# Third stage of a four-stage transformer chain: how half of the attention weights are turned, and when they meet the values

## The chip, the cores and the metric

The kernel runs on one core of one Trainium2 chip. The metric is the device time of one execution in microseconds (us), the median of several. The core has a matrix engine (TensorE, PE), a vector engine (VectorE, DVE), a scalar engine (ScalarE, ACT), a general engine (GpSimd, POOL) and a queue that issues the transfers (SyncE, SP). Each works through its own list of instructions in order and waits on semaphores for the others.

## The reference, cut to what matters

2048 tokens (16 x 128) of width 512 pass through four stages, each of the form x = x + gate * block(layernorm(x)): a latent attention, a gated FFN with low-rank experts, a causal attention, and a mixture of low-rank maps. The change lies in the third:

```python
def _L1_xattn_ref(q, latent_kv, Wq, Wkv_expand, Wout):      # q: layernorm(x); 16 heads of 32
    qp = q @ Wq.T
    k, v = jnp.split(latent_kv @ Wkv_expand.T, 2, axis=-1)
    scores = jnp.einsum('bhqd,bhkd->bhqk', qh, kh) * inv_sqrt_d
    scores = jnp.where(causal, scores, jnp.finfo(scores.dtype).min)
    attn = jax.nn.softmax(scores, axis=-1)
    out = jnp.einsum('bhqk,bhkd->bhqd', attn, vh)
    return out @ Wout.T
```

Each of the 16 sequences has 128 tokens, so the scores of a head and a sequence are one 128x128 square. The value product needs that square with the keys on the partitions, that is, turned.

## The kernel before, in words

The tokens are worked in four tiles m of 512 (four sequences b each). In the third stage the 16 heads are four groups g of four heads j, and a **unit** u = 4m + g is one group of heads for one tile: 16 units. The stage is a loop over u from 0 to 17 that stands in each engine's program, with the work of unit u spread over passes u to u + 2. What one pass u holds, in TensorE's order:

- `scores3(u-1)`: 16 small products into banks 4 to 7 (one bank a head, four sequences in it). The causal mask must be in the bank first. In the passes after u = 3, 4, 5, 6, 10 and 14 (and the first ones) TensorE puts it there itself with 4 products (`mkb,idb` in the profile). For the others it is "seeded": ACT or DVE copies it into the bank as soon as its exponentials are done (`seed3`, `seeded(u)`).
- `q3(u)` (12 products), then in passes 6, 10, 14 `v3(m)` (12), then the output projection of finished tokens, `wo3`, 12 products a block: one block where g = 3 or 1, two where g = 0 (`wo_at(u)`; from pass 7).
- `turn3(u-2)`: 16 transpositions of P, head by head, into four banks taken from the ring of banks 0 to 3 (`ring3`); then `k3(u)` (3 products), `ln_turn` (transpositions of the next tokens) and `cx_turn`.
- `av3(u-2)`: the value product, 16 small products on PT3, the copy of the turned P in SBUF.

The other engines in the same pass. DVE: `largest(u-1, j)`, four maxima straight from the score banks; `q3_out(u)`; the low half of `av3(u-3)`; two `inverse`; seeds of heads 0 and 1 (where g = 1, head 0 alone); `v3`; `final3` for each `wo3` block; `turn3` copies of heads 0 and 1; `inverse`; `k3(u)`; `ln_pre`, `ln_turn` and `cx_turn` low halves; the last `inverse`. ACT: `exp3(u-1)`, 16 exponentials (four a head), the remaining seeds, `turn3` copies of heads 2 and 3 (ahead of the last head's exponentials or of its seed), `ln_turn` and `cx_turn` high halves, the high half of `av3(u-2)`. POOL: `norm3(u-1, j)`, which multiplies P by the inverse sums, `rstd_of`, `ln_norm` (the layer norm of tokens for the next tile) and `w4_split`. SP: loads of tokens and of the fourth stage's weights (`w4`, through six slots of the staging buffer STG), loads and stores of the third stage's output rows.

`scores3(u)` waits for `q3` and `k3` of its unit to be copied out (Q3 and K3 are single buffers), and for the score banks to be free, which the last exponential or the last seed does. No planner is involved: the order is written out in each engine's function. In the trace all products carry line 118 and transpositions 121, copies 127 (DVE, POOL) and 124 (ACT), `largest` 146, `inverse` 149, `ln_pre` 152, 155 and 136, `ln_norm` 137, 32x32 block turns 164, transfers 170. MSK holds Q3 and K3, PTV holds PT3 and the values, AR and XT the split operands.

The first stage already turns its P in another way: DVE turns every 32x32 block (line 164), the result goes to the DRAM scratch `pscr` and comes back with the blocks moved by four transfers (PYZ is the buffer at both ends).

## Time and profile before

| | us |
|---|---|
| median of 3 runs | 1375.35 (1373.85 to 1378.79) |
| the profiled execution | 1376.7 |
| its span in the trace | 1374.9, so 1.8 lie around it |
| third stage, passes 1 to 17 | from about 1028 to 1223 |
| PE, DVE, ACT, POOL busy over the span | 98%, 68%, 38%, 31% |
| granted TensorE clock | 0.997 of full |

The scores of each pass start in the trace at these times (from pass 4 on the pass is full; 17 has none, and its first product starts at 1212.10):

| pass | 3 | 4 | 5 | 6 | 7 | 8 | 9 | 10 | 11 | 12 | 13 | 14 | 15 | 16 |
|---|---|---|---|---|---|---|---|---|---|---|---|---|---|---|
| us | 1049.01 | 1059.53 | 1068.96 | 1078.60 | 1091.15 | 1102.30 | 1115.49 | 1126.27 | 1138.79 | 1149.92 | 1163.09 | 1173.88 | 1186.38 | 1197.09 |

A busy share is an average over stages with different limits. For the third stage the table by stretches, one a pass, and the chain of waits say more than the shares of the whole span.

### The profile page before, as it was taken

Reading aid. Unit: us, or ns where it says so; the run is one execution under the profiler, and the core shown is the slowest. Engines: PE = TensorE matmul, PEld = TensorE weight load, DVE = VectorE, ACT = ScalarE, POOL = GpSimd, SP = SyncE. Lnnn points to the kernel's source line nnn. Section 1 sums busy time; section 2 is a strip of 40 time slices with the busy share of each in tenths; the row PEclk is TensorE's granted clock in tenths of the full one; section 3 lists DMA queues with packets and bytes.
Section 4 is the critical chain, followed back from the end, with each engine's and each line's share of the span. In section 5 each row is a group of like instructions: output and inputs, shape, how many; then the busy total and the mean of one; then the engine's idle time right before and its main releaser. Section 6 shows DMA issues by size and latency. Waiting matters only on the chain.

```text
span 1374.9 us, 20467 instructions
## 1 busy us (share of the span) xinstructions
PE 1348.0 (98%) x7596; PEld 1091.5 (79%) x7596; DVE 929.3 (68%) x1787; ACT 518.5 (38%) x1569; POOL 422.1 (31%) x463
## 2 busy tenths in 40 slices
PE   7899999999999999999999999999999999999999
PEld 6688888888778788878887888788876788887787
DVE  5565675666674877786678667776988777845533
ACT  2544455445464331231113111311127777822220
POOL 3123433233254443101111112113427865630000
PEclk9999999999999999999999999999999999999999
DMA  8633434433454322210121112112334031144431
GB/s 282 222 124 101 148 124 130 131 123 116 135 149 120 92 85 77 88 47 20 43 88 31 51 39 85 43 46 69 106 102 136 28 129 62 47 139 153 139 123 54
DMA packets 108615, 138.35 MB, mean 101 GB/s; under 512 B 12876, under 2 KB 66252, under 8 KB 108516
## 3 DMA queue, kind: packets, MB, share of 16 engines
q1 hardware_dynamic: 108516, 137.05, 31.3%
q8 instruction: 60, 0.98, 0.3%
q14 instruction: 39, 0.32, 0.1%
HBM read 97.15 MB, written 39.85 MB: 100 GB/s over the span
## 4 chain that ended last, share of the span: by engine, by line
PE 81%; DVE 9%; DMA 5%; ACT 2%; issue 1%; SPq 1%; POOL 1%; DVEq 0%; ACTq 0%; POOLq 0%
PE bank L118 78%; PE bank L121 4%; DMA PYZ<-pscr 2%; DMA pscr<-PYZ 2%; SPq L170 1%; DVE PYZ L164 1%; DVE XR L140 1%; DVE AH L130 1%; DVE STG L130 1%; DVE AH L127 1%; DVE st L152 1%; ACT Pb L124 1%; ACT PT L124 1%; DMA XR<-scr 0%; DVE XR L137 0%
## 5 line engine op out<-in xcount | busy, mean ns | idle before, releaser
L118 PE MATMUL bank<-XT,AR 128*128 128x512 f32 x1152 | 280.2, 393 | 0.1
L118 PE MATMUL bank<-AR 128*128 128x512 f32 x1056 | 260.6, 396 | 3.2 <-DVE Msb L127 2.3
L118 PEld LDWEIGHTS bank<-XT,AR 128*128 128x128 f32 x1152 | 213.9, 188 | 48.3 <-issue 1.5
L124 ACT ACTIVATE STG<-bank,b1c 128x512 f32<-128x512 f32 x128 | 88.3, 690 | 387.7 <-PE bank L118 317.7
L118 PEld LDWEIGHTS bank<-AR 128*128 128x128 f32 x1056 | 193.7, 188 | 48.2 <-DVE Msb L127 2.7
L118 PE MATMUL bank<-AR,CT 128*128 128x512 f32 x768 | 192.7, 394 | 0.0
L118 PE MATMUL bank<-AR,AH 128*128 128x512 f32 x768 | 185.9, 390 | 0.0
L127 DVE CAST AH<-STG 128x512 fp32r<-128x512 f32 x192 | 93.8, 488 | 110.5 <-PE bank L118 96.4
L118 PEld LDWEIGHTS bank<-AR,AH 128*128 128x128 f32 x768 | 143.7, 188 | 30.7 <-issue 1.1
L118 PEld LDWEIGHTS bank<-AR,CT 128*128 128x128 f32 x768 | 140.0, 188 | 27.2 <-issue 0.4
L127 POOL CAST BA<-STG 128x256 fp32r<-128x256 f32 x64 | 31.4, 490 | 396.4 <-PE bank L118 242.8
L130 DVE TENSOR_TENSOR AH<-STG,AH 128x512 fp32r<-128x512 f32 x192 | 140.5, 732 | 6.6
L124 ACT ACTIVATE Pb<-bank,sm 128x128 f32<-128x128 f32 x256 | 90.0, 377 | 122.3 <-DVE sm L136 122.3
L130 POOL TENSOR_TENSOR Pb<-Pb,sm 128x512 f32<-128x512 f32 x64 | 66.6, 1042 | 185.3 <-DVE sm L149 185.3
L118 PE MATMUL bank<-TM,BA 128*128 128x512 f32 x384 | 107.5, 392 | 1.0 <-POOL BA L130 0.4
L124 ACT ACTIVATE P<-bank,sm 128x128 f32<-128x128 f32 x256 | 90.1, 395 | 31.9 <-DVE sm L146 31.9
L118 PE MATMUL bank<-AH,BA 128*128 128x512 f32 x384 | 97.5, 389 | 0.0
L130 POOL TENSOR_TENSOR rstd<-ve,mhalf 128x1 f32<-128x1 f32 x64 | 49.1, 771 | 148.6 <-DVE ve L136 148.5
L130 DVE TENSOR_TENSOR STG<-STG 128x512 f32<-128x512 f32 x128 | 89.6, 700 | 4.2
L130 POOL TENSOR_TENSOR P<-P,sm 128x512 f32<-128x512 f32 x64 | 65.4, 1043 | 75.8 <-DVE sm L149 75.8
L118 PEld LDWEIGHTS bank<-TM,BA 128*128 128x128 f32 x384 | 71.4, 188 | 19.0 <-ACT STG L124 2.2
L118 PEld LDWEIGHTS bank<-AH,BA 128*128 128x128 f32 x384 | 72.1, 188 | 15.4
(139 smaller groups left out, 1839.3 us busy)
## 6 DMA issues: line engine op xcount, KB each, us to landing
XR<-scr SPq DMA_DIRECT2D x64, 256.0 KB, 2.9
pscr<-PYZ SPq DMA_DIRECT2D x30, 512.0 KB, 2.9
PYZ<-pscr SPq DMA_DIRECT2D x120, 128.0 KB, 2.9
XR<-in_x_dram SPq DMA_DIRECT2D x32, 256.0 KB, 3.6
scr<-XR SPq DMA_DIRECT2D x32, 256.0 KB, 2.1
STG<-in_WoT_dram SPq DMA_DIRECT2D x8, 512.0 KB, 3.9
STG<-in_Wq_dram SPq DMA_DIRECT2D x8, 512.0 KB, 4.9
STG<-in_W1L_dram SPq DMA_DIRECT2D x16, 256.0 KB, 2.7
```

The lines of the kernel that those rows point to most:

```text
L118: return self.e.matmul(o, w, x, start=start, stop=stop, skip_group_check=True) if self.e else Nothing()
L121: return self.e.transpose(o, x, ident) if self.e else Nothing()
L124: return self.e.activation(o, x, func, **kw) if self.e else Nothing()
L127: return self.e.tensor_copy(o, x) if self.e else Nothing()
L130: return self.e.tensor_tensor(out=o, in0=a, in1=b, op=op) if self.e else Nothing()
L140: return self.e.scalar_tensor_tensor(out=o, in0=a, scalar=s, in1=b, op0=op0, op1=op1) if self.e else Nothing()
L152: return self.e.bn_stats(o, x) if self.e else Nothing()
L164: return self.e.transpose(o, x) if self.e else Nothing()
L170: return self.e.dma_start(o, x) if self.e else Nothing()
```

## The change

1. Heads 0 and 1 of each unit are no longer turned by TensorE. At the start of DVE's pass u, ahead of the maxima, `turn_p3(u-2)` turns the 32x32 blocks of P of both heads into P3Y, 1024 columns of the staging buffer (it waits there for `norm3` of both). SP stores P3Y to `pscr` and loads it back in four transfers into P3Z, the first 1024 columns of PTV. The load waits for the value product of the unit before, since P3Z is single, and both stand at the start of SP's pass, ahead of its other transfers.
2. TensorE's and DVE's `turn3` keep 8 transpositions a unit and none of the copies of heads 0 and 1; ACT's two copies remain, and stand ahead of the last head's exponentials in passes 6, 10 and 14 as elsewhere.
3. The value product of unit u-3 (`av3(u-3)`) is issued in pass u behind `q3(u)`, before it was that of unit u-2 at the end of pass u. ACT takes its high half behind the exponentials of heads 0 and 1, DVE its low half behind the seeds. For heads 0 and 1 it reads P3Z in four runs of 32 columns.
4. The two token tiles (2, 1, 0) and (2, 1, 1) are normalised by DVE in pass 2 in place of POOL in pass 1.
5. P3Y takes the place of two weight slots, so the `w4` loads rotate over four.

```diff
+        P3Y, P3Z = STG[:, 2048:3072], PTV[:, 0:1024].rearrange("p (j n c) -> p n j c", j=4, n=8)
...
             def turn3(u, ring):
-                for b in range(4):
+                for b in (2, 3):
...
             def av3(u, ring):
                 for b in range(4):
-                    pe.wait_ge(*ps.drained(("pt3", u, b)))
                     pe.wait_ge(*ps.drained(("v3", m, b)))
+                pe.wait_ge(*d_p3[u, 3])
+                pe.wait_ge(*ps.drained(("pt3", u, 2)))
+                pe.wait_ge(*ps.drained(("pt3", u, 3)))
...
+                        if j < 2:
+                            ins = pe.matmul(o.rearrange("p (a c) -> p a c", a=4), V3[:, b, 32 * h:32 * h + 32],
+                                            P3Z[:, 4 * j + b], True, True)
...
             # TensorE, pass u
                 if 1 <= u < 16:
                     q3(u, ring3)
+                if u >= 3:
+                    av3(u - 3, ring3)
...
-                if u >= 2:
-                    av3(u - 2, ring3)
+            av3(15, ring3)
...
             # ScalarE, pass u
                 if 1 <= u <= 16:
                     exp3(u - 1, (0, 1))
+                if u >= 3:
+                    av3(u - 3)
...
             # VectorE
+            def turn_p3(u):
+                for j in range(2):
+                    e.wait_ge(*nm3_ok[u, j])
+                    if u:
+                        e.wait_ge(*t_p3[u - 1])
+                    e.turn(blocks_out(P3Y)[:, 4 * j:4 * j + 4],
+                           blocks_in(P3[:, u % 2, 0:1024])[:, 4 * j:4 * j + 4]).then_inc(*p3y_ok.mark((u, j)))
...
+                if u >= 2:
+                    turn_p3(u - 2)
                 if 1 <= u <= 16:
                     for j in range(4):
                         largest(u - 1, j)
...
+                if u == 2:
+                    ln_norm(2, 1, 0)
+                    ln_norm(2, 1, 1)
...
-                if u >= 2:
-                    turn3(u - 2, 0)
-                    turn3(u - 2, 1)
...
             # SyncE
+            def p3_store(u):
+                e.wait_ge(*p3y_ok[u, 1])
+                if u >= 2:
+                    e.wait_ge(*d_p3[u - 2, 3])
+                e.dma(pscr[u % 2], P3Y).then_inc(*t_p3.mark(u))
+
+            def p3_load(u):
+                e.wait_ge(*t_p3[u])
+                if u:
+                    e.wait_ge(*ps.full(("av", u - 1)))
+                src = pscr[u % 2].rearrange("(j r) (i x) -> i r j x", j=4, i=4)
+                for k in range(4):
+                    e.dma(PTV[32 * k:32 * k + 32, 0:1024].rearrange("r (j x) -> r j x", j=4), src[k]).then_inc(*d_p3.mark((u, k)))
```

TensorE, passes 8 (g = 0) and 9 (g = 1) up to the scores of pass 10, before:

```order
700 L118 MATMUL bank<-MSK 128x128 x16
701 L118 MATMUL bank<-AR 128x512 x36
702 L121 MATMUL bank<-ident,P 128x128 x16
703 L118 MATMUL bank<-AR 128x512 x3
704 L118 MATMUL bank<-PTV 32x128 x16
705 L118 MATMUL bank<-MSK 128x128 x16
706 L118 MATMUL bank<-AR 128x512 x24
707 L121 MATMUL bank<-ident,P 128x128 x16
708 L118 MATMUL bank<-AR 128x512 x3
709 L121 MATMUL bank<-ident,XR 128x128 x4
710 L118 MATMUL bank<-PTV 32x128 x16
711 L118 MATMUL bank<-MSK 128x128 x16
```

The same, now:

```order
701 L118 MATMUL bank<-MSK 128x128 x16
702 L118 MATMUL bank<-AR 128x512 x12
703 L118 MATMUL bank<-PTV 32x128 x16
704 L118 MATMUL bank<-AR 128x512 x24
705 L121 MATMUL bank<-ident,P 128x128 x8
706 L118 MATMUL bank<-AR 128x512 x3
707 L118 MATMUL bank<-MSK 128x128 x16
708 L118 MATMUL bank<-AR 128x512 x12
709 L118 MATMUL bank<-PTV 32x128 x16
710 L118 MATMUL bank<-AR 128x512 x12
711 L121 MATMUL bank<-ident,P 128x128 x8
712 L118 MATMUL bank<-AR 128x512 x3
713 L121 MATMUL bank<-ident,XR 128x128 x4
714 L118 MATMUL bank<-MSK 128x128 x16
```

The value product (PTV) stood between `k3` (the x3) and the scores (MSK); now `k3` stands next to the scores of the next pass where g = 0, and the value product lies behind `q3`.

VectorE, the second half of pass 9 up to the maxima of pass 10, before (MSK at line 127 is the copy of `k3`, lines 152 to 136 the statistics of `ln_pre`):

```order
1170 L127 COPY PTV<-bank 128x512 x2
1171 L149 RECIPROCAL sm<-sm 128x4
1172 L127 COPY MSK<-bank 128x512
1173 L152 BN_STATS st<-XR 128x6
1174 L155 BN_AGGR mv<-st 128x2
1175 L136 TENSOR_SCALAR ve<-mv 128x1
1176 L152 BN_STATS st<-XR 128x6
1177 L155 BN_AGGR mv<-st 128x2
1178 L136 TENSOR_SCALAR ve<-mv 128x1
1179 L130 TENSOR_TENSOR AR<-bank,AR 128x4x128
1180 L149 RECIPROCAL sm<-sm 128x4
1181 L146 TENSOR_REDUCE sm<-bank 128x4 x4
```

The same, now:

```order
1172 L149 RECIPROCAL sm<-sm 128x4
1173 L127 COPY MSK<-bank 128x512
1174 L152 BN_STATS st<-XR 128x6
1175 L155 BN_AGGR mv<-st 128x2
1176 L136 TENSOR_SCALAR ve<-mv 128x1
1177 L152 BN_STATS st<-XR 128x6
1178 L155 BN_AGGR mv<-st 128x2
1179 L136 TENSOR_SCALAR ve<-mv 128x1
1180 L130 TENSOR_TENSOR AR<-bank,AR 128x4x128
1181 L149 RECIPROCAL sm<-sm 128x4
1182 L164 STREAM_TRANSPOSE STG<-P 128x4x4x32 x2
1183 L146 TENSOR_REDUCE sm<-bank 128x4 x4
```

Two copies went from the middle of the pass, and two block turns came in between the last inverse and the next maxima.

ScalarE, pass 9 (mkb is a seed, PTV a copy of the turned P), before and then now:

```order
314 L124 ACTIVATE P,sm<-bank,sm 128x128 x16
315 L124 ACTIVATE bank<-mkb 128x512 x2
316 L124 ACTIVATE PTV<-bank 128x512 x2
317 L124 ACTIVATE bank<-mkb 128x512
318 L124 ACTIVATE XT<-bank 128x4x128
319 L124 ACTIVATE AR<-bank 128x512
```

```order
321 L124 ACTIVATE P,sm<-bank,sm 128x128 x8
322 L124 ACTIVATE AR<-bank 128x512
323 L124 ACTIVATE P,sm<-bank,sm 128x128 x8
324 L124 ACTIVATE bank<-mkb 128x512 x2
325 L124 ACTIVATE PTV<-bank 128x512 x2
326 L124 ACTIVATE bank<-mkb 128x512
327 L124 ACTIVATE XT<-bank 128x4x128
```

The high half of the value product (AR, 128x512) moved from the end of the pass into the middle of the exponentials, ahead of the seeds.

## Rows read from the trace of the kernel before

**Rows 1.** The page's first part: busy time, share of the span, instructions.

```profile
PE 1348.0 (98%) x7596; PEld 1091.5 (79%) x7596; DVE 929.3 (68%) x1787; ACT 518.5 (38%) x1569; POOL 422.1 (31%) x463
```

**Rows 2.** Stretches of passes 8, 9, 11: length, busy PE, PEld, DVE, ACT, POOL.

```profile
1102.30:1115.49 13.19, 13.09 (x124) 10.79 (x120) 9.61 (x19) 8.37 (x37) 5.98 (x6) 1.00 0.24 85
1115.49:1126.27 10.78, 10.78 (x115) 9.03 (x111) 8.55 (x20) 9.32 (x39) 8.55 (x8) 1.00 0.24 78
...
1137.83:1149.92 12.09, 12.09 (x123) 9.75 (x120) 9.68 (x20) 9.45 (x39) 8.32 (x8) 1.00 0.19 70
```

**Rows 3.** TensorE by time, pass 9: start, us, line, operation, count, idle before.

```profile
1115.49 1.17 PE L118 MATMUL bank<-MSK 32*128 32x128 f32 x32
1116.59 3.04 PE L118 MATMUL bank<-XT,AR 128*128 128x512 f32 x12
1119.47 2.89 PE L118 MATMUL bank<-AR 128*128 128x512 f32 x12
1122.19 1.91 PE L121 MATMUL bank<-ident,P 128*128 128x128 f32 x16
1123.87 0.96 PE L118 MATMUL bank<-AR 128*128 128x512 f32 x3
...
1125.26 1.08 PE L118 MATMUL bank<-PTV 128*32 128x128 f32 x32
1126.27 1.17 PE L118 MATMUL bank<-MSK 32*128 32x128 f32 x32
```

**Rows 4.** ScalarE by time, pass 9.

```profile
1117.40 0.37 ACT L124 ACTIVATE P<-bank,sm 128x128 f32<-128x128 f32 x1 [1.19 <-DVE sm L146]
...
1122.91 1.21 ACT L124 ACTIVATE bank<-mkb 128x512 f32<-128x512 bf16 x2
1123.95 1.17 ACT L124 ACTIVATE PTV<-bank 128x512 f32<-128x512 f32 x2
1124.90 0.70 ACT L124 ACTIVATE bank<-mkb 128x512 f32<-128x512 bf16 x1
1125.42 0.70 ACT L124 ACTIVATE AR<-bank 128x512 fp32r<-128x512 f32 x1
```

**Rows 5.** VectorE by time, pass 9 and the maxima of pass 10.

```profile
1116.68 2.48 DVE L146 TENSOR_REDUCE sm<-bank 128x4 f32<-128x512 f32 x4 [0.49 <-PE bank L118]
...
1123.13 1.28 DVE L127 COPY PTV<-bank 128x512 f32<-128x512 f32 x2
...
1124.86 0.69 DVE L127 COPY MSK<-bank 128x512 f32<-128x512 f32 x1 [0.37 <-PE bank L118]
1125.47 0.68 DVE L152 BATCH_NORM_STATS2 st<-XR 128x6 f32<-128x512 f32 x1
...
1128.16 2.45 DVE L146 TENSOR_REDUCE sm<-bank 128x4 f32<-128x512 f32 x4
```

**Rows 6.** VectorE by time, first stage: the same two block turns.

```profile
54.19 1.30 DVE L164 STREAM_TRANSPOSE PYZ<-Pb 128x512 f32<-128x512 f32 x2
```

**Rows 7.** TensorE by time: first and last scores of the table, two early waits.

```profile
1046.47 0.63 PE L121 MATMUL bank<-ident,XR 128*128 128x128 f32 x4 [1.44 <-POOL XR L137]
...
1049.01 1.17 PE L118 MATMUL bank<-MSK 32*128 32x128 f32 x32
...
1065.05 1.09 PE L121 MATMUL bank<-ident,P 128*128 128x128 f32 x8 [0.51 <-DVE AR L130]
...
1197.09 1.17 PE L118 MATMUL bank<-MSK 32*128 32x128 f32 x32
```

**Rows 8.** Layer norm instructions (line 137), whole span: ns least/median/most.

```profile
L137 DVE TENSOR_SCALAR XR<-XR,mv,rstd x48: 504/539/1568, 6.0 to 1302.6; 128x512 f32<-128x512 f32 x48
L137 POOL TENSOR_SCALAR XR<-XR,mv,rstd x16: 2079/2084/2092, 1042.2 to 1188.3; 128x512 f32<-128x512 f32 x16
```

**Rows 9.** Chain of waits, first stage, an early unit: start, us, what.

```profile
41.59 6.09 DMA pscr<-PYZ
...
49.02 2.92 DMA PYZ<-pscr
```

**Rows 10.** The tile PYZ and its scratch: time to landing of all transfers.

```profile
DMA to landing us min/median/max: 2.4/2.9/6.9
```

More of the change, by code:

```diff
@@ L353, in build @@
         t_ly = sig("t_ly", 16)
+        t_p3, d_p3 = sig("t_p3", 16), sig("d_p3", 16)
         def kinds(count, names):
@@ L363, in build @@
         vy_ok, vz_ok, py_ok, pz_ok, ly_ok, lz_ok = kinds(on_dve, "vy_ok vz_ok py_ok pz_ok ly_ok lz_ok")
+        (p3y_ok,) = kinds(on_dve, "p3y_ok")
         c_mh, c_sel, rs_ok, kvc_rd, kvr_ok, kvl_ok = kinds(on_pool, "c_mh c_sel rs_ok kvc_rd kvr_ok kvl_ok")
@@ L412, in build, with normed_by_pool @@
                 xr_take("ln", 3, m, tb)
-        normed_by_pool = ((2, 1), (2, 2), (2, 3), (3, 0))
+        def normed_by_pool(ph, m, tb):
+            return (ph, m) in ((2, 1), (2, 2), (2, 3), (3, 0)) and (ph, m, tb) not in ((2, 1, 0), (2, 1, 1))
         def xr_ap(*key):
@@ L562, in ln_turn @@
                 pe.wait_ge(*ps.free(key))
-                pe.wait_ge(*(xp_ok if (ph, m) in normed_by_pool else xn_ok)[ph, m, tb])
+                pe.wait_ge(*(xp_ok if normed_by_pool(ph, m, tb) else xn_ok)[ph, m, tb])
                 for c in range(4):
@@ L986, in av3 @@
                         h = 4 * g + j
-                        ins = pe.matmul(k[32 * j:32 * j + 32, 128 * b:128 * b + 128], V3[:, b, 32 * h:32 * h + 32],
-                                        PT3[:, 512 * j + 128 * b:512 * j + 128 * b + 128], True, True)
+                        o = k[32 * j:32 * j + 32, 128 * b:128 * b + 128]
+                        if j < 2:
+                            ins = pe.matmul(o.rearrange("p (a c) -> p a c", a=4), V3[:, b, 32 * h:32 * h + 32],
+                                            P3Z[:, 4 * j + b], True, True)
+                        else:
+                            ins = pe.matmul(o, V3[:, b, 32 * h:32 * h + 32],
+                                            PT3[:, 512 * j + 128 * b:512 * j + 128 * b + 128], True, True)
                 ins.then_inc(*ps.fill(("av", u)))
@@ L1388, in exp3 @@
                     if u >= 2:
-                        ac.wait_ge(*ps.full(("pt3", u - 2, j)))
+                        ac.wait_ge(*(p3y_ok[u - 2, j] if j < 2 else ps.full(("pt3", u - 2, j))))
                     for b in range(4):
@@ L1421, in h4 @@
                         ac.wait_ge(*ps.full(("pt3", 14, 3)))
+                        ac.wait_ge(*p3y_ok[14, 1])
                         ac.wait_ge(*d_c4[3])
@@ L1445, in scalar @@
                     turn3(u - 2, 3)
+                if values:
+                    exp3(u - 1, (3,))
                 if seeded(u):
@@ L1456, in scalar @@
                     cx_turn(m + 1)
-                if u >= 2:
-                    av3(u - 2)
+            av3(15)
             def logits(m):
@@ L1890, in inverse @@
                 e.recip(S[:, 4:8], S[:, 4:8]).then_inc(*rc_ok.mark(("3", u, j)))
-            def turn3(u, b):
-                e.wait_ge(*ps.full(("pt3", u, b)))
-                if u:
-                    e.wait_ge(*ps.full(("av", u - 1)))
-                e.copy(PT3[:, 512 * b:512 * b + 512], ps.ap(("pt3", u, b))[:, :]).then_inc(*ps.drain(("pt3", u, b), on_dve))
+            def turn_p3(u):
[5 more added lines that the diff above has]
+                           blocks_in(P3[:, u % 2, 0:1024])[:, 4 * j:4 * j + 4]).then_inc(*p3y_ok.mark((u, j)))
             def av3(u):
@@ L1928, in vector @@
                         seed3(u, j)
+                if u >= 3:
+                    av3(u - 3)
                 if u > 4 and g == 2:
@@ L2198, in w4_split @@
                 kind, c, hi, lo, _ = w4[n]
-                e.wait_ge(*d_slot[n % 6]["w4", n])
+                e.wait_ge(*d_slot[n % 4]["w4", n])
                 if kind == "U":
                     e.wait_ge(*ps.full(("w3", 2, 3)))
-                split(hi, lo, slots[n % 6]).then_inc(*w4_ok.mark((kind, c)))
+                split(hi, lo, slots[n % 4]).then_inc(*w4_ok.mark((kind, c)))
             for u in range(18):
@@ L2216, in gpsimd @@
                         rstd_of(2, 1, tb)
-                    for tb in tiles3(u)[g]:
-                        ln_norm(2, 1, tb)
                 for n in w4_step.get(u, ()):
@@ L2449, in xf_store @@
                 e.dma(rows(3, m, tb), XF[:, tb, :]).then_inc(*t_xf[tb].mark(m))
+            def p3_store(u):
[10 more added lines that the diff above has]
+                    e.dma(PTV[32 * k:32 * k + 32, 0:1024].rearrange("r (j x) -> r j x", j=4), src[k]).then_inc(*d_p3.mark((u, k)))
             for u in range(18):
                 m, g = divmod(u, 4)
+                if u >= 2:
+                    p3_store(u - 2)
+                    p3_load(u - 2)
                 for tile in (ln3_tiles(u) if u < 16 else ()):
@@ L2457, in sync @@
                 for n in w4_step.get(u, ()):
-                    if n >= 6:
-                        e.wait_ge(*w4_ok[w4[n - 6][0:2]])
+                    if n >= 4:
+                        e.wait_ge(*w4_ok[w4[n - 4][0:2]])
                     elif n < 2:
@@ L2463, in sync @@
                         e.wait_ge(*ps.drained(("acc2", 3, 3)))
-                    e.dma(slots[n % 6], w4[n][4]).then_inc(*d_slot[n % 6].mark(("w4", n)))
+                    e.dma(slots[n % 4], w4[n][4]).then_inc(*d_slot[n % 4].mark(("w4", n)))
                 if u > 4 and g == 2:
```

5 lines of the change are left out of this document (removed).

## The prediction

> **What bounds the kernel now.** TensorE is busy 98% of the span [rows 1]. I read the third stage by stretches next: a pass of 13.19 us holds 13.09 of TensorE, one of 10.78 holds 10.78, one of 12.09 all of it, with DVE, ACT and POOL at 8 to 10 [rows 2]. So on paper it is TensorE's, and what is taken from it counts in full. But the busy times of ACT and DVE hide that they form a loop with TensorE, and how close that loop is decides this case. In pass 9 it runs: scores at 1115.49 [rows 3]; maxima 1.19 later, at 1116.68 [rows 5]; exponentials from 1117.40, 0.72 behind the maxima, to 1122.91, so 5.51 for 16; two seeds 1.04; two copies of the turned P 0.95; the last seed from 1124.90 to 1125.60 [rows 4]. Only then are the banks free for the next scores, which start at 1126.27 [rows 3]: the loop has 0.67 us to spare. Here the next maxima start 1.89 behind their scores, not 1.19 [rows 5]: DVE is late already.
>
> **What TensorE is relieved of.** 16 transpositions take 1122.19 to 1123.87, 1.68 us; seen with what follows, 0.105 each [rows 3]. Eight fewer give 0.84 a unit, 13.4 for 16 units. The value product (1.01, from 1125.26 to 1126.27 [rows 3]) moves and stays the same length if four runs of 32 columns stream like one of 128. No row shows that form: at the least it costs nothing, at the most each of the 8 small products takes twice as long, 0.5 a unit or 8 in all. I take nothing, since even at contiguous P 32 of these small steps take 1.08 [rows 3], so they run side by side and one that reads slower has cover. Two waits lie in passes 2 to 4 too: 1.44 for POOL's layer norm, and 0.5 in each of three passes for the bank of the value product [rows 7]; both lose their cause, 1.4 and 1.5. Were TensorE the bound throughout, the gain would be 13.4 + 2.9 = 16.3.
>
> **What is put on the loop.** On DVE the two copies (1.28) leave the middle of the pass [rows 5], where they shortened no wait; two block turns, 1.30 [rows 6], come in directly ahead of the maxima. As work this is even; as a place it is not. On ACT the high half of the value product, about 0.5 (the like instruction at 1125.42 is one [rows 4]), comes from the end of the pass into the loop. And TensorE's value product no longer stands between `k3` and the next scores: the copy of `k3` ends at 1125.55, 1.68 behind the start of `k3` at 1123.87 [rows 3, 5], and the scores need it.
>
> The Trainium skill (page VectorE: DVE Perf Modes, "The three transpose paths" and the rules for kernel authors) advises TensorE for a 128x128 transposition whose target may be PSUM, and VectorE for 32x32 blocks; it gives 390 ns against 311 for bf16. The rows differ from that as a choice for this kernel: 105 ns of TensorE's path against 1.30 / 8 = 163 ns of DVE for a square. An estimate from its figures would have a unit give 3.1 us back for 2.5 on DVE, over 16 units some 50 us less on TensorE, which no row here bears out; the trace decides, 0.84 for 1.3.
>
> **The loop worked out.** Let L be the start of the maxima, F the time when the score banks are free. In a pass with g = 1 and seeds, F = L + 0.72 + 5.51 + 0.5 + 1.04 + 0.95 + 0.7 = L + 9.4. With g = 3 one seed less, L + 8.9. In passes 3 to 5, without seeds, L + 7.7; where `v3` is (6, 10, 14) ACT has two more copies, L + 8.8; in both the scores start at F + 0.3, behind TensorE's own mask, else at F + 0.1. The next L: after F, ACT takes the high half of the turned tokens (0.6, 1.1 or 1.6 for one, two or three tiles), DVE the low half (0.65), the inverse (0.1) and now the block turns (1.3): F + 2.65, 3.1 or 3.6, and F + 1.45 with no tile. The earliest L is 1.19 behind the scores. With g = 0 and seeds (8, 12) TensorE has two projection blocks and ACT waits for it: `k3` starts 11.1 behind the scores before, + 1.0 - 0.84 = 11.3 now, the copy ends at 13.0, and that is the pass; 13.19 before [rows 2]. The next L stands behind that copy by 1.0 for one tile's statistics (2.69 for two of them, a low half and an inverse, from 1125.47 to 1128.16 [rows 5]), 0.1 and 1.3: 2.4 after the scores.
>
> Carried through, from the pass table, scores after against before: pass 3 at 1048.05 (-1.0: the waits of pass 2 go, the last exponential then bounds it), 4 at 1058.8 (-0.8), 5 at 1070.1 (+1.1, since three turned tiles made pass 4's maxima late), 6 at 1079.7 (+1.1), 7 at 1091.2 (0), 8 at 1103.0 (+0.7), 9 at 1116.0 (+0.5), 10 at 1127.9 (+1.6), 11 at 1139.6 (+0.8), 12 at 1151.4 (+1.5), 13 at 1164.4 (+1.3), 14 at 1176.3 (+2.4), 15 at 1188.0 (+1.6), 16 at 1199.8 (+2.7) [first and last of before in rows 7]. One of these in full: pass 9 starts at 1116.0, L = 1118.4, F = 1127.8, scores at 1127.9, against 10.78 a pass before; pass 10: L = 1127.8 + 2.65 = 1130.5, F = 1139.3, scores at 1139.6, where TensorE before needed 12.5 for masks, `v3` and turns: what pass 9 loses, pass 10 gives back in part. Passes 16 and 17 have no scores behind them and are TensorE's: -0.84 each. Sum: +2.7 - 1.7 = **+1.0 us**.
>
> **What stays hidden.** The layer norm on DVE, 0.5 each and 1.57 at worst against 2.08 on POOL [rows 8], lies in pass 2 and is in the -1.0; at worst it takes that back. The worst is a row beside a busy POOL, and the Trainium skill (SBUF — State Buffer, "A bandwidth-pool intuition that's wrong") has it that one of the two blocks fully while the other holds the shared port; the trace agrees (504 to 1568 ns for one form). The transfers: store 6.1 at most in the chain, four issues about 1.4, landing 2.9, together 10.4 [rows 9]; from L to the value product of the next pass there are 11.5 in pass 3 and 13 to 15 later. SP's other transfers now stand behind `p3_load`, some 5 us into the pass; what they load is wanted one pass later. The slots fall from six to four, but a slot is reused four passes later, after its split. The last unit: its turns lie at about 8 in pass 16, landed at 19, wanted at 23.
>
> **Rivals.** *TensorE stays the bound.* If L is not late (POOL and ACT tails shorter than I add them), g = 1 gives 10.65, g = 2 and 3 save 0.9 each and g = 0 0.2, two of the early passes 1 each: -7 to -10, to the full -16.3: 1359 to 1368. For it: TensorE's busy share; against it: `inverse` of the last head and the low halves stand ahead of the turns in DVE's list, and maxima already start late. *The transfers are late.* Slower: the landing ranges up to 6.9 [rows 10], which makes the way 6.1 + 1.4 + 6.9 = 14.4; the point from which it decides is 13.4 in a full pass and 11.5 in passes 3 to 5. At 14.4 twelve passes wait 1.0 and three 2.9: +20, 1396; with half of them late +10, 1386. Against it: the median is 2.9. *POOL holds the turns.* They wait for `norm3` of two heads, and POOL has two layer norms (2.08 each [rows 8]) and a weight split in some passes; where it is behind, DVE waits ahead of the maxima. Under 0.2 a pass it is lost in the sum; at 0.75 in each of the 11 passes that the loop bounds it is +8, 1384. *The change does nothing here* is the forecast itself: the gain is made on TensorE and lost behind the maxima.
>
> **How the numbers follow.** The span goes from 1374.9 to 1375.9; with 1.8 around it 1377.7 against the profiled 1376.7. That execution was 1.35 above the median, so I put the forecast at 1375.35 + 1.0 = 1376.4. Chances: the loop as worked out 0.52 (its own range, 0.35 a pass either way over 14 passes, 1371 to 1381), TensorE bound 0.28, the two slower ones 0.10 each. Half a per cent, about what a measurement can tell here, is 6.9 us: faster 0.28, same 0.52, slower 0.20. The range takes in 1364 to 1385.
>
> **What would show it.** After: passes of 11.5 to 12 us with g = 1 and 3, of 13.0 with g = 0; TensorE idle ahead of scores, released by ACT's seed or the `k3` copy; maxima 2 to 3 us behind their scores; busy TensorE down by some 13 while the span stands. TensorE without idle time, or maxima at 1.2, would make it wrong on the fast side; a value product that waits for a transfer into PTV, on the slow side.

## The result, and the profile after

| kernel | median of the time | runs | ratio to before, 95% interval |
|---|---|---|---|
| before | 1376.08 us | 7 | |
| changed | 1383.02 us (1381.25 to 1384.89) | 7 | 1.0050 (1.0037 to 1.0064) |

The changed kernel is 6.9 us slower. Its profiled execution has a span of 1381.2 us, 6.3 more than before's 1374.9. The page's busy line of the changed kernel, to be read beside [rows 1]:

```profile
PE 1339.4 (97%) x7468; PEld 1077.7 (78%) x7468; DVE 929.5 (67%) x1789; ACT 516.1 (37%) x1569; POOL 418.2 (30%) x461
```

TensorE is busy 8.6 us less and ends 6.3 us later: it idles some 15 us more. Passes 8, 9 and 11 of the changed kernel, each from its scores to the next (length, then busy PE, PEld, DVE, ACT, POOL). They stand against [rows 2], whose third row, though, begins with the masks ahead of pass 11's scores; from scores to scores pass 11 took 11.13 us before:

```profile
1105.39:1118.77 13.38, 12.44 (x111) 9.82 (x112) 9.88 (x20) 9.21 (x39) 5.96 (x6) 1.00 0.52 179
1118.77:1130.47 11.70, 10.08 (x104) 8.07 (x104) 9.25 (x22) 8.95 (x39) 8.54 (x8) 1.00 0.47 158
1142.45:1154.00 11.55, 10.74 (x109) 8.46 (x108) 9.07 (x18) 8.83 (x40) 7.33 (x7) 1.00 0.60 213
```

Before, TensorE was busy 10.78 of 10.78 us in pass 9. Now it is busy 10.08 of 11.70. What ends its idle time there, TensorE by time in pass 9 of the changed kernel (compare [rows 3]):

```profile
1118.77 1.17 PE L118 MATMUL bank<-MSK 32*128 32x128 f32 x32 [0.87 <-DVE MSK L127]
1119.88 3.01 PE L118 MATMUL bank<-XT,AR 128*128 128x512 f32 x12
1122.82 1.08 PE L118 MATMUL bank<-PTV 128*32 128x128 f32 x32
1123.83 3.02 PE L118 MATMUL bank<-AR 128*128 128x512 f32 x12
1126.69 1.03 PE L121 MATMUL bank<-ident,P 128*128 128x128 f32 x8
1127.48 0.94 PE L118 MATMUL bank<-AR 128*128 128x512 f32 x3
1128.25 0.60 PE L121 MATMUL bank<-ident,XR 128*128 128x128 f32 x4
1130.47 0.79 PE L118 MATMUL bank<-MSK 32*128 32x128 f32 x17 [1.61 <-ACT bank L124]
```

Two waits stand there that were not there before: the scores that begin the pass wait 0.87 for VectorE's copy of the keys (K3, tile MSK), and the scores that end it 1.61 for ScalarE's seed of a score bank. VectorE ahead of those scores, and ScalarE at the end of the same pass (compare [rows 4, 5]):

```profile
1117.93 0.69 DVE L127 COPY MSK<-bank 128x512 f32<-128x512 f32 x1 [0.66 <-PE bank L118]
...
1119.63 1.28 DVE L164 STREAM_TRANSPOSE STG<-P 128x512 f32<-128x512 f32 x2
1120.83 2.44 DVE L146 TENSOR_REDUCE sm<-bank 128x4 f32<-128x512 f32 x4
```

```profile
1127.50 1.22 ACT L124 ACTIVATE bank<-mkb 128x512 f32<-128x512 bf16 x2
1128.54 1.18 ACT L124 ACTIVATE PTV<-bank 128x512 f32<-128x512 f32 x2
1129.49 0.72 ACT L124 ACTIVATE bank<-mkb 128x512 f32<-128x512 bf16 x1
1130.01 0.71 ACT L124 ACTIVATE AR<-bank 128x512 fp32r<-128x512 f32 x1
```

The maxima start 2.06 us behind their scores (1.19 before), directly behind the block turns. The last seed is out 9.4 us behind the start of the maxima, and the scores start at 9.6. The four largest waits of TensorE over the third stage (1036.9 to 1228.1) of the changed kernel, 16.2 of 18.4 us: what waited, for whom, sum, times, longest:

```profile
PE bank L118 <- ACT P L124: 6.3, 7, 2.0
PE bank L118 <- ACT bank L124: 5.4, 5, 1.6
PE bank L121 <- ACT PTV L124: 2.7, 4, 1.3
PE bank L118 <- DVE MSK L127: 1.8, 2, 0.9
```

Before, the same view of its third stage has three entries, 3.6 us together:

```profile
PE bank L121 <- DVE AR L130: 1.5, 3, 0.5
PE bank L121 <- POOL XR L137: 1.4, 1, 1.4
PE bank L118 <- DVE PTV L127: 0.7, 1, 0.7
```

The transfers are no part of this. No wait names them, and they land as those of the first stage do (compare [rows 10]); the page's rows of issues, with median us to landing:

```profile
pscr<-STG SPq DMA_DIRECT2D x16, 512.0 KB, 2.6
PTV<-pscr SPq DMA_DIRECT2D x64, 128.0 KB, 2.8
```

One more thing happened, in pass 5. TensorE by time, and then four stretches of it (the number ahead of the DMA share is the granted clock, 1.00 being the 2.4 GHz level and 0.50 the 1.2 GHz level):

```profile
1067.64 0.39 PE L118 MATMUL bank<-mkb,idb 128*128 128x512 bf16 x1 [1.03 <-ACT P L124]
1070.01 0.39 PE L118 MATMUL bank<-mkb,idb 128*128 128x512 bf16 x1 [1.98 <-ACT P L124]
1070.33 1.67 PE L118 MATMUL bank<-MSK 32*128 32x128 f32 x32
1071.93 4.11 PE L118 MATMUL bank<-AR 128*128 128x512 f32 x12
```

```profile
1068.00:1070.00 2.00, 0.03 (x1) 0.00 (x0) 1.32 (x5) 1.96 (x10) 0.92 (x1) 1.00 0.96 287
1071.00:1072.00 1.00, 1.00 (x21) 0.78 (x17) 0.38 (x2) 0.00 (x0) 0.90 (x3) 0.50 0.00 0
1073.00:1074.00 1.00, 1.00 (x4) 0.81 (x3) 1.00 (x3) 1.00 (x7) 1.00 (x2) 0.50 0.59 217
1075.00:1076.00 1.00, 1.00 (x9) 0.55 (x8) 0.00 (x0) 0.63 (x4) 0.94 (x1) 1.00 0.00 0
```

After two waits of 1.03 and 1.98 us the clock fell to the lower level for about 3.4 us: the scores took 1.67 instead of 1.17, the query products 4.11 instead of 3.02, so 1.6 us were lost on top of the wait. It is not a matter of this one execution: behind the same wait of 1.98 us ahead of pass 5 the clock fell in the profiles of experiments 2, 3 and 8 too, and not in that of 5. The kernel before has no fall in its third stage.

### The profile page after: what moved, and what is told of

It reads as the page before. It is cut to its first block, busy times and chain, and to the rows that moved or that the text cites. A ratio compares the mean times of both kernels' runs of the same rounds, so it can differ in the third digit from the quotient of the medians.

```text
span 1381.2 us, 20251 instructions
## 1 busy us (share of the span) xinstructions
PE 1339.4 (97%) x7468; PEld 1077.7 (78%) x7468; DVE 929.5 (67%) x1789; ACT 516.1 (37%) x1569; POOL 418.2 (30%) x461
## 4 chain that ended last, share of the span: by engine, by line
PE 73%; DVE 10%; ACT 8%; DMA 5%; issue 2%; SPq 1%; POOL 0%; DVEq 0%; ACTq 0%; POOLq 0%
PE bank L118 72%; ACT P L124 4%; PE bank L121 2%; DMA PYZ<-pscr 2%; SPq L170 1%; DMA pscr<-PYZ 1%; ACT PTV L124 1%; DVE PYZ L164 1%; DVE XR L140 1%; DVE AH L130 1%; DVE STG L130 1%; DVE STG L164 1%; DVE st L152 1%; ACT Pb L124 1%; DVE AH L127 1%
```

## The experiments

All are read by two measures. The time (median, ratio to before) decides what is faster. But one profile scatters: the scores of pass 2 start between 1032.9 and 1038.9 us, and from the first logits of stage four to the end it is 151.5 to 156.7 us. So the mechanism is read from the **third stage** of each profile, in two parts: from the scores of pass 2 to those of pass 16, and from there to the first logits. That is 160.05 + 26.14 us before and 165.69 + 25.39 in the changed kernel. The last columns are the lengths of four passes of the steady part. Each ratio is to runs of the kernel before made beside that experiment; their medians lie between 1375.34 and 1376.18. All in us:

| kernel | time | ratio (95%) | passes 2 to 15 | 16 to logits | pass 8 | 9 | 10 | 11 |
|---|---|---|---|---|---|---|---|---|
| before | 1376.08 | | 160.05 | 26.14 | 13.19 | 10.78 | 12.52 | 11.13 |
| changed | 1383.02 | 1.0050 (1.0037 to 1.0064) | 165.69 | 25.39 | 13.38 | 11.70 | 11.98 | 11.55 |
| 1 product moved alone | 1381.10 | 1.0037 (1.0021 to 1.0052) | 163.87 | 27.21 | 14.14 | 11.42 | 12.51 | 11.43 |
| 2 without transfers | 1382.29 | 1.0054 (1.0034 to 1.0073) | 167.88 | 25.39 | 13.39 | 11.69 | 11.98 | 11.54 |
| 3 turns a pass earlier | 1384.60 | 1.0060 (1.0044 to 1.0076) | 169.77 | 25.39 | 13.38 | 11.72 | 13.59 | 10.74 |
| 4 idle time filled once | 1383.25, one run | | 165.68 | 25.37 | 13.39 | 11.69 | 13.59 | 11.54 |
| 5 turns last | 1375.96 | 1.0005 (0.9992 to 1.0018) | 157.51 | 29.66 | 13.38 | 11.34 | 12.00 | 10.63 |
| 6 turns last, keys first | 1373.53 | 0.9983 (0.9967 to 0.9999) | 150.69 | 29.97 | 13.26 | 10.38 | 11.30 | 10.42 |
| 7 keys first | 1377.43 | 1.0015 (1.0002 to 1.0028) | 159.36 | 25.72 | 13.53 | 10.71 | 12.21 | 10.78 |
| 8 norms back | 1382.81 | 1.0055 (1.0036 to 1.0073) | 167.43 | 25.39 | 13.38 | 11.67 | 11.98 | 11.53 |
| 9 as 6, trimmed | **1366.06** | **0.9927 (0.9908 to 0.9946)** | 149.85 | 25.52 | 12.46 | 10.37 | 11.53 | 10.41 |
| 10 no turns, keys first | 1393.66 | 1.0126 (1.0106 to 1.0146) | 174.51 | 27.17 | 14.58 | 12.31 | 13.56 | 12.68 |
| 11 as 10, key copy early | 1375.56 | 0.9996 (0.9984 to 1.0008) | 158.59 | 27.16 | 13.22 | 10.87 | 12.49 | 11.36 |
| 12 as 9, norms back | 1369.67 | 0.9943 (0.9928 to 0.9959) | 153.07 | 25.52 | 13.38 | 10.39 | 11.35 | 10.41 |

### 1. The value product moved alone

The kernel before, with the product's new place on TensorE, ScalarE and VectorE; all sixteen squares stay on TensorE. As in the change, ScalarE's two copies of turned P stand ahead of the last head's exponentials in passes 6, 10 and 14 too; passes 10 and 14 keep their lengths within 0.01 us, and pass 6 is 0.19 shorter, so this is not what costs time. TensorE's part:

```diff
                 if 1 <= u < 16:
                     q3(u, ring3)
+                if u >= 3:
+                    av3(u - 3, ring3)
...
-                if u >= 2:
-                    av3(u - 2, ring3)
+            av3(15, ring3)
```

> The kernel before with one part of the change: the value product of unit u-3 behind q3 of pass u on TensorE, its halves on ScalarE and VectorE at the places of the change; all 16 transpositions and copies stay, no block turns, no transfers. Loop theory: what hurts is the block turns ahead of the maxima; the move alone exposes the copy of k3 in passes 8 and 12 (+0.65 each), and puts 0.5 on ScalarE's loop, whose maxima are early again without the turns: +1 to +3 us on before. Rival (the move itself is the loss): +6 to +7, as much as the whole change.

Measured: +5.4 us over the 1375.73 of before beside it, third stage 191.08, as long as the changed kernel's. TensorE's three largest waits in it:

```profile
PE bank L118 <- DVE MSK L127: 3.1, 5, 0.9
PE bank L121 <- POOL XR L137: 1.4, 1, 1.4
PE bank L118 <- ACT P L124: 1.2, 2, 0.8
```

The product used to stand between the key product and the next scores, and hid VectorE's copy of the keys. Without it the copy is exposed, 3.1 us. And pass 16 to the logits takes 27.21 against 26.14, 1.07 more: one value product more lies behind the last scores. The expectation of +1 to +3 was too low. So the move alone costs 4.9 us of the third stage, though the maxima of pass 9 start 1.16 us behind their scores, early. What the rest of the change adds there, block turns above all, is zero on balance in these two profiles.

### 2. No transfers

The changed kernel, with the block turns written to two buffers that the value product reads directly. The 80 transfers are left out, and so is their work of putting the blocks of two heads in place.

```diff
-                pe.wait_ge(*d_p3[u, 3])
+                pe.wait_ge(*p3y_ok[u, 1])
...
-                if u >= 2:
-                    p3_store(u - 2)
-                    p3_load(u - 2)
```

> The change without its 80 transfers: the block turns write two buffers in turn and the value product reads them as they are, so the blocks of heads 0 and 1 stand at the wrong places in the sum and the output differs; every other instruction is kept. Loop theory: nothing waited for a transfer into PTV, so the third stage takes the same time, 0 to -1.5 us on the change (the fourth stage's start may be a little earlier): 1381.5 to 1383. Rival (the transfers, or the traffic and SP's queue behind them, are the loss): about 7 back, 1376.

Measured: 1382.29, and passes 8 to 11 are those of the changed kernel to 0.01 us. Passes 2 to 15 are 2.2 us longer in this profile; the clock was at its lower level for about 3.5 us in each of passes 3, 5 and 14, and pass 14 took 13.59 us instead of 12.00. The transfers cost the changed kernel nothing that can be seen.

### 3. The turns one pass earlier

```diff
-                if u >= 2:
-                    turn_p3(u - 2)
...
+                if 1 <= u <= 16:
+                    turn_p3(u - 1)
```

The new call stands behind the layer norm's statistics and ahead of the low halves, where I took VectorE for idle.

> The change with one thing moved: VectorE's block turns of a unit stand one pass earlier, behind the statistics and ahead of the low halves of the turned tokens, where VectorE waits for ScalarE anyway, and not ahead of the maxima. Same instructions on every engine. Loop theory: 1.2 us leaves the loop in some ten passes; passes with g = 1 fall from 11.7 to about 10.8, with g = 3 from 11.6 to about 10.4, with g = 2 to TensorE's own 11.7, g = 0 stays 13.3: third stage 10 to 14 us shorter than in the change, time 1368 to 1373. Rival (VectorE's work counts, not its place): 1383 as the change.

Measured: 1384.6, where 1368 to 1373 had been expected. The turns were still ahead of the maxima (maxima 2.5 us behind their scores in pass 10), and now they could meet P before GpSimd had normalised it. VectorE's wait for that:

```profile
DVE STG L164 <- POOL P L130: 4.8, 5, 3.0
```

Passes 7, 11 and 15 did get 0.5 to 0.8 us shorter. What was lost lies in pass 2 (2.1 us longer), pass 4 (2.9) and pass 10, where the clock fell behind a wait of 1.63. I take it that the end of the pass is not where VectorE has time, but the middle, while the exponentials run; experiment 5 tries that.

### 4. TensorE kept busy ahead of pass 5

The changed kernel with twelve repeated mask products in the idle time ahead of pass 5's scores.

```diff
+                        if u == 4 and j in (1, 2):
+                            for _ in range((0, 4, 8)[j]):
+                                pe.matmul(blocks3(ks[0]), idb[:, :], mask3, True, False)
```

> The change with 12 repeated mask products into a bank that holds only its mask, in the 3 us of pass 4 to 5 in which TensorE stood idle. Theory of the clock: behind that idle time the granted clock fell to 0.50 for about 4 us and the scores and q3 of pass 5 took 1.67 and 4.11 us where they take 1.17 and 3.02 elsewhere; with the engine kept busy the clock stays at 1.00 there, q3 takes 3.0, and pass 5 is 1.5 to 2 us shorter. Rival (the slow q3 comes from operands or the transfers at that time): q3 still takes 4.1.

Measured: the scores took 1.17, the query products 3.02 and pass 5 9.95 us instead of 11.53, so 1.58 of that pass was the clock. But the third stage is as long as ever. In pass 2 the clock fell too, which pass 3 gave back, and pass 10 took 13.59 instead of 11.98:

```profile
1127.60 1.17 PE L118 MATMUL bank<-MSK 32*128 32x128 f32 x32 [1.60 <-ACT bank L124]
1128.70 4.61 PE L118 MATMUL bank<-XT,AR 128*128 128x512 f32 x12
```

```profile
1130.00:1131.00 1.00, 1.00 (x3) 0.73 (x3) 1.00 (x3) 0.22 (x1) 1.00 (x3) 0.50 0.00 0
```

The clock fell behind the idle time of another pass. The changed kernel's profile has the same wait there (1.61) and no fall. So the loss to the clock is real, but its place changes, and filling one gap doesn't cure it: there are others. This rests on one execution.

### 5 to 7. The order of the pass

Experiment 5 moves the turns of the changed kernel behind the query copy (`q3_out`), experiment 7 puts TensorE's key product ahead of the remaining transpositions of P and ScalarE's two copies behind its last exponential and seed, and 6 does both. No run separates the two moves of 7.

VectorE, in 5 and 6:

```diff
-                if u >= 2:
-                    turn_p3(u - 2)
                 if 1 <= u <= 16:
                     for j in range(4):
                         largest(u - 1, j)
                 if 1 <= u < 16:
                     q3_out(u)
+                if u >= 2:
+                    turn_p3(u - 2)
```

TensorE, in 6 and 7:

```diff
+                if 0 < u < 16:
+                    k3(u, ring3)
                 if u >= 2:
                     turn3(u - 2, ring3)
-                if 0 < u < 16:
-                    k3(u, ring3)
```

ScalarE, in 6 and 7:

```diff
+                if 1 <= u <= 16 and not project:
+                    exp3(u - 1, (3,))
+                if seeded(u):
+                    seed3(u, 3)
                 if u >= 2:
                     turn3(u - 2, 2)
                     turn3(u - 2, 3)
-                if values:
-                    exp3(u - 1, (3,))
-                if seeded(u):
-                    seed3(u, 3)
-                if 1 <= u <= 16 and not project and not values:
-                    exp3(u - 1, (3,))
```

> The changed kernel with one edit: VectorE's eight block turns of unit u-2 stand behind the third query copy of unit u (at the end of the pass) and no longer ahead of unit u's maxima. Nothing else is moved. Theory A (the pass is a loop maxima, exponentials, score banks free, next scores; the turns' 1.30 us lie in front of the maxima only where VectorE comes late to them, and behind the query copy they lie in idle time of VectorE): up to 1.2 us a pass leaves the loop, the third stage becomes 8 to 11 us shorter than in the changed kernel, 1372 to 1376 us. Rival B (the passes are bound by TensorE's and ScalarE's own work, wherever VectorE's turns stand): within 1.5 us of the changed kernel, 1381 to 1384. Rival C (the turned blocks now land too late, since their transfers leave some 9 us later in the pass): the transposed value product waits for PTV, more than 1 us in most passes, 1385 or more.

> The previous experiment (turns at the end of the pass) with two more moves: on TensorE the third key product of unit u stands ahead of the remaining probability transposition of unit u-2, and ScalarE's two copies of transposed probabilities stand behind its last exponential. Theory A: the key copy is then no longer exposed in the passes of the first head (0.88 us of waits of the scores in each) and the score banks come free about 1.0 us earlier in every pass; TensorE's own work becomes the bound nearly everywhere, third stage 12 to 20 us shorter than in the changed kernel, 1362 to 1370 us. Rival B (ScalarE's copies, now late, hold up the value product as much as they did the scores): within 2 us of the previous experiment, whatever that is.

> The changed kernel with only the two moves on TensorE and ScalarE: the third key product ahead of the remaining probability transposition, and ScalarE's two copies of transposed probabilities behind its last exponential. VectorE's turns stay ahead of the maxima. Theory A (exposed key copy, and copies in front of exponentials): 3 to 6 us faster than the changed kernel, 1377 to 1380 us. Rival B (the maxima alone set the pass): within 1 us of the changed kernel, 1382 to 1384.

Measured: 5 is 7.1 us faster than the changed kernel (6.2 by the ratios to before), a time inside the expected range. Its maxima start 1.17 us behind the scores in pass 9, no longer 2.06, and its passes 2 to 15 are 8.2 shorter. Of these 4.8 lie in passes 2 to 5, 1.57 of them in pass 5, where this time the clock did not fall; from pass 7 on the passes with g = 1 and 3 gain 0.3 to 0.9 each. The whole third stage is only 3.9 shorter, where 8 to 11 had been expected, since what is behind the scores of pass 16 grew by 4.3. 7 is 5.6 faster (4.8 by the ratios), passes 2 to 15 shorter by 6.3 and the third stage by 6.0, as expected. Its pass 9 took 10.71 us although the maxima still start 2.06 behind the scores; with both edits (6) it took 10.38. So in that order the late maxima cost little. 6 has both: passes 2 to 15 shorter by 15.0, the third stage by 10.4, where 12 to 20 had been expected, and no wait for a key copy or a seed left in passes 8 to 11. Its time of 1373.53 beats the kernel before by 0.17%, with an interval that just excludes no change, but misses the 1362 to 1370 expected. What kept it back, TensorE by time in its trace:

```profile
1095.17 3.00 PE L118 MATMUL bank<-XT,AR 128*128 128x512 f32 x12 [0.76 <-DVE XT L130]
...
1187.80 1.93 PE L118 MATMUL bank<-PTV 128*32 128x128 f32 x32 [3.01 <-DMA PTV<-pscr]
...
1294.66 1.12 PE L121 MATMUL bank<-ident,XR 128*128 128x128 f32 x4 [3.24 <-DVE XR L137]
```

ScalarE's late copies now delay the turned context in front of the query product (0.76). In pass 16 there is no query product, so the value product comes earlier than its transfer, which now starts later: 3.01 us of waiting (2.63 in 5) and the lower clock behind it, the product taking 1.93 instead of 1.08. That is the rival of late transfers after all, in one pass: 29.97 and 29.66 us from pass 16 to the logits against 25.39. The third wait lies in the fourth stage. It was 0.96 before and 1.55 in the changed kernel, and 3.24 and 3.42 in experiments 6 and 7, behind token loads that were issued 2.4 and 2.8 us later after the first logits than before. Why is open: experiment 9, whose fourth stage is the same, waited 1.4 in all, and 12 again 4.4.

### 8. Layer norms back on GpSimd

```diff
-            return (ph, m) in ((2, 1), (2, 2), (2, 3), (3, 0)) and (ph, m, tb) not in ((2, 1, 0), (2, 1, 1))
+            return (ph, m) in ((2, 1), (2, 2), (2, 3), (3, 0))
...
-                if u == 2:
-                    ln_norm(2, 1, 0)
-                    ln_norm(2, 1, 1)
```

> The changed kernel with the two layer norms of pass 1 given back to GpSimd (part four of the change undone). Theory: scores of pass 3 come 1.0 to 2 us later than in the changed kernel, and half of it or more is taken up by the passes behind, so 1383 to 1385 us. Rival (the two on VectorE cost elsewhere what they gain there): 1381 to 1382.5.

Measured: pass 2 took 12.15 us instead of 11.06, as the theory has it; the times, 1382.81 and 1383.02, can't tell the two apart, and 1382.81 lies between what the theory and its rival had. On VectorE the two took 0.98 together. See 12.

### 9. Experiment 6, trimmed

Context and layer norm are transposed ahead of the probabilities in passes 7, 11 and 15 (TensorE, and ScalarE's copies likewise), and pass 16 has its value product behind the two output blocks.

```diff
-                if u >= 3:
+                if u >= 3 and u != 16:
                     av3(u - 3, ring3)
...
                 for block in wo_at(u):
                     wo3(*block)
+                if u == 16:
+                    av3(13, ring3)
                 if 0 < u < 16:
                     k3(u, ring3)
-                if u >= 2:
+                if u >= 2 and (u == 3 or g != 3):
                     turn3(u - 2, ring3)
...
                     cx_turn(m + 1, ring3)
+                if u > 3 and g == 3:
+                    turn3(u - 2, ring3)
```

> The kernel with the turns at the end of the pass and the key product first, and two edits more: in passes 7, 11 and 15 TensorE's and ScalarE's turns of the context and the layer norm stand ahead of the remaining probability transposition; in pass 16 the value product of unit 13 stands behind the two output blocks, on TensorE and on VectorE. Theory: of the waits left in its trace 0.76 and 0.78 us in front of query products (<-DVE XT, AR) and 3.01 us in pass 16 (<-DMA PTV), with the slower clock behind that one, go: third stage 4 to 6 us shorter than there (180.7 us from the scores of pass 2 to the logits), 1368 to 1371 us. Rival (something else in the fourth stage takes up what is gained, as it did 5 us of it in that trace): within 1 us of 1373.5.

Measured: 1366.06, 10 us faster than the kernel before, 17 than the changed one and 7.5 than experiment 6; more than expected. The third stage gained 5.3, as expected, most of it in pass 16 and behind it, 25.52 instead of 29.97. The rest of the 7.5 can't be laid to the edit: the fourth stage, which it doesn't touch, was 5.2 us shorter in this profile than in that of 6. The page's busy line, and then the stretches of passes 8 and 9:

```profile
PE 1335.7 (98%) x7468; PEld 1077.8 (79%) x7468; DVE 928.3 (68%) x1789; ACT 516.5 (38%) x1569; POOL 417.4 (31%) x461
```

```profile
1098.57:1111.03 12.46, 12.36 (x113) 9.92 (x112) 9.84 (x20) 9.32 (x41) 6.73 (x8) 1.00 0.65 201
1111.03:1121.40 10.37, 10.07 (x104) 8.11 (x104) 8.71 (x20) 8.65 (x39) 8.92 (x9) 1.00 0.49 176
```

TensorE is the bound again, 12.36 of 12.46 in pass 8, and the work taken off it now counts.

### 10 and 11. The same order without block turns

Experiment 1 with the key product first and ScalarE's copies last, all 16 squares on TensorE (10); then VectorE's copy of the keys ahead of its two copies of turned P as well (11). The edit that 11 adds:

```diff
+                if 1 < u < 16:
+                    k3(u)
                 if u >= 2:
                     turn3(u - 2, 0)
                     turn3(u - 2, 1)
                 if 1 <= u <= 16:
                     inverse(u - 1, 2)
-                if 1 < u < 16:
-                    k3(u)
```

> The kernel with the value product alone moved (all sixteen 128x128 squares still turned by TensorE, no block turns and no transfers of P), plus the third key product ahead of the probability transposition and ScalarE's two copies behind its last exponential. It stands to the kernel with the turns last and the keys first as a kernel without the block turns. Theory A (with the loop cured, TensorE's own work is the bound, and the block turns then save what they take off it, 14 turns of 1.03 us or half of a pass's probability transposition of 2.08): third stage 8 to 14 us longer than there, 1378 to 1384 us. Rival B (the turns are worth nothing even then; the move and the order make all the difference): 1372 to 1375 us.

> The previous kernel without block turns (all 16 squares on TensorE, product moved, key product first, ScalarE's copies last) with one edit: VectorE copies the third keys ahead of its two copies of turned P and no longer behind them. In the trace of that kernel TensorE waited 14 times, 17.0 us in all, 1.17 us each in most, for the bank that the key copy held, ahead of its fourth group of transpositions. Theory (those waits were that order and nothing else): they go, third stage some 15 us shorter than there, 1376 to 1381 us, and the block turns are then worth the difference to 1373.5 of the kernel with them, 3 to 7 us. Rival (the last two copies then hold the next scores or the fourth group anyway): 1386 or more.

Measured: 10 is 1393.66, slower than either theory had it. TensorE in pass 8 of 10:

```profile
1118.76 1.47 PE L121 MATMUL bank<-ident,P 128*128 128x128 f32 x12
1121.40 0.66 PE L121 MATMUL bank<-ident,P 128*128 128x128 f32 x4 [1.17 <-DVE MSK L127]
```

The fourth group of transpositions needs the bank that the keys are still in. VectorE copies the keys only behind two copies that wait for the transpositions. In all, 17.0 us in 14 waits. Copied earlier (11), they cost nothing: 1375.56, the time of before (1375.57 beside it). Against 11, experiment 6 with the block turns has passes 2 to 15 shorter by 7.9 us and gives 2.8 back behind the scores of pass 16. But 6 also has the two layer norms on VectorE, and 1.3 of the 7.9 lie in pass 2, where these count (experiments 8 and 12); that leaves 6.6 for the block turns in passes 2 to 15. Trimmed (9) it is 8.7 and a time 9.5 lower, with the trimming and the norms in it; experiment 12, trimmed and without the norms, is 5.9 below 11. So the order alone undoes the damage of the move, and the runs that come below the kernel before have the block turns in them. A trimmed order without block turns was not tried.

### 12. The trimmed kernel with the norms on GpSimd

The edit of 8, made to 9.

> The fastest kernel so far (trimmed passes, 1366.1) with both layer norms of pass 1 back on GpSimd. Theory: pass 2 becomes 1.1 us longer, as it did in the changed kernel (12.15 against 11.06), and since TensorE is now the bound of nearly every pass nothing behind takes it up: 1366.8 to 1368. Rival (worth nothing, as the times of the changed kernel with and without it could not tell apart): 1365.5 to 1366.5.

Measured: 1369.67, 3.6 us slower than 9, more than expected. Pass 2 is 1.27 longer (10.84 against 9.57), as the theory has it; passes 3 to 15 are 1.9 longer, 1.4 of it where pass 5's value product waited for its transfer. So the cover over the transfers is thin in this order. What of the 3.6 is the norms' own beyond the 1.27 is open; the fourth stage was 4.6 us longer in this profile than in that of 9.

## Why the prediction was right, and where it was not

The forecast, 1376.4 with no change the likeliest, is 6.6 us low. The time lies inside the stated range of 1364 to 1385, and the ratio of 1.0050 lies on the bound of half a per cent that divides no change from slower. But it lies 2 us above the range of the loop theory itself, 1371 to 1381: it is the width left for the rivals that takes it in, and that is luck. Nor did the span stand still, as "what would show it" had it. I count the mechanism that was worked out as right but incomplete, and the sum as wrong.

- **TensorE's relief** was put at 13.4; its busy time fell by 8.6. In pass 9, 16 squares took 1.68 us on the path before [rows 3], and 8 take 0.79 now (1126.69 to 1127.48): 0.89 for the forecast 0.84. That is 14 us over 16 units, and the busy time fell 5 less; 1.6 of these are the slower clock of pass 5, and ahead of the scores of pass 2, where TensorE's program is the same, it is busy 1.0 longer in this execution. The rest isn't traced. The runs of 32 columns cost nothing: 1.08 for the value product, half of which reads them, as before.
- **The loop** was right in place and size. Forecast: maxima 2.4 behind the scores, banks free 9.4 later, passes of 11.5 to 12 with g = 1 and 3, 13.0 with g = 0. Measured: 2.06, 9.4, 11.55 to 11.70, 13.38. The releasers are the two that were named, ScalarE's seed (5.4 us) and the key copy (1.8), and, with the largest sum (6.3), ScalarE's last exponentials where no seed is put: the same loop, in passes 2, 4, 5, 6, 10 and 14. Scores of pass 3 were forecast at 1048.05 and came at 1048.02, of pass 4 at 1058.8 and 1058.88.
- **The sum** of +1.0 at the logits became +4.8. The steps: up to the scores of pass 5, +0.2. In pass 5, +1.9, of which 1.58 is the clock; I had counted waits of TensorE at their length, and they cost more (experiment 4). In passes 6 to 15, +0.7: two passes of 13.38 and 13.37 stand where I had 13.0. And +0.95 at the end: I credited the shift of the value product in pass 2 and forgot that the last one then comes behind the last scores, 1.07 in experiment 1. That was arithmetic, and could have been seen from the diff.
- **Behind the logits** 1.5 us more, 153.2 against 151.7, from two waits for layer norms. Kernels with the same fourth stage took between 151.5 (9) and 156.7 (6), so I can't lay this at the change.
- **What carried the loss.** "The gain is made on TensorE and lost behind the maxima" is half of it. By experiment 1 the move of the value product alone costs all 4.9 us of the third stage, where the prediction's reasoning, applied to it before that run, gave +1 to +3; in that order the block turns bring TensorE no more than they take in their place. The two losses overlap: to cure the turns' place alone (5) took 7.1 us off, the two moves of 7 alone took 5.6, and both together 9.5.
- **Layer norm on VectorE:** forecast -1.0 at pass 3 in all, measured 1.09 by experiment 8 and 1.27 by 12. The two took 0.98, at the lower end of [rows 8]. Experiment 1, with both norms on GpSimd, has pass 2 at 10.85 us, though, and the changed kernel 11.06: without the block turns the move of the value product alone brings what was forecast at pass 3.
- **The rivals.** Late transfers fell by experiment 2, for the changed kernel; with the turns later in the pass they did come, in pass 16 (5, 6). GpSimd holding the turns did not occur in the changed kernel (no block turn had idle time before it), and did in experiment 3, 4.8 us. TensorE as the bound, 1359 to 1368, did not happen as written, and is what experiment 9 reaches: 1366.06 from the same replaced work in another order. The forecast had the price of this change right in kind, and did not say that the price hung on the place.

On the choice of engine for a turn: the Trainium skill (VectorE: DVE Perf Modes, "Rules for kernel authors") would have VectorE for 32x32 blocks and TensorE for a 128x128 turn where the target may be PSUM. The estimate of 50 us from the figures of its section "The three transpose paths" shows in no run. In like orders (6 and 11) the turns taken off TensorE were worth at most 6.6 us over passes 2 to 15.

## What to carry to other kernels

When an instruction is moved, ask what it was hiding where it stood: here the value product covered a copy that the next scores need, and nothing in the busy times says so. When work goes to an engine with idle time, put it where that engine waits for the others, not ahead of the step for which they wait: the same two block turns cost some 7 us more ahead of the maxima than in the gap behind them, the slower clock included. In this kernel the relief of the bounding engine was cashed in only when the order around it was cured too.

## What the chip showed unexpectedly

- Idle TensorE time can cost more than its length: behind waits of 1.03 and 1.98 us the granted clock stood at 0.50 for about 3.4 us, worth 1.58 us in pass 5. It is not certain to: behind the 1.98 it fell in four profiles (the changed kernel, 2, 3, 8) and not in a fifth (5), and behind a wait of 1.60 in one execution (4) and not behind 1.61 at the same place in another.
- Moving the 1.08 us value product of each unit, without adding any work, cost 4.9 us in all; reordering one VectorE copy was worth 18.1 us (10 against 11), since it held a bank of TensorE's once in nearly every pass (14 waits, 17.0 us).
- The value product took 1.08 us whether or not the moving operand of half its small products lay in four runs of 32 columns.
